# Attention maps of a two-layer transformer kernel: from one map at a time to pairs of maps in row and column groups of TensorE

## The reference, cut to what matters

```python
# HEADS 16, HD 4, per batch b, head h and side s (cut to its core)
S      = (q[b,h,s] @ k[b,h,s].T) * HD ** -0.5          # 1024 x 1024, contraction over 4
A[s]   = softmax(S, axis=-1)
out    = A[0] @ v[b,h] - lam * (A[1] @ v[b,h])          # v is 1024 x 8
out    = rms_norm(out) * w * (1 - LAMBDA_INIT)
x      = x + gate * (concat_heads(out) @ w_proj.T + b_proj)
```

## Time and profile before

| quantity | value |
|---|---|
| median of 3 runs | 3686.81 us (3684.1 to 3694.66) |
| the profiled execution: its time | 3684.8 us |
| the profiled execution: its span in the trace | 3683.0 us |
| mean granted clock of TensorE over the span | 0.962 of full speed |
| first max matmul of the attention maps | 89.15 us |
| last weighing matmuls of the attention maps | up to 1108.7 us |
| first matmul of `join_maps` | 1126.76 us |
| last step of `join_maps` | 1199.10 us |

### The profile page before, as it was taken

How to read it: one execution, slowest core, us unless ns; L and a number is a source line. 1 busy time by engine, 2 the same in 40 slices (tenths; PEclk the granted TensorE clock), 3 DMA queues, 4 the chain that set the end, 5 groups by cost and what they waited for, 6 DMA issues and landing times. The chain is left out here.

```text
span 3683.0 us, 71336 instructions
## 1 busy us (share of the span) xinstructions
PE 3280.8 (89%) x25164; PEld 1821.2 (49%) x25164; DVE 2741.0 (74%) x3715; ACT 2013.3 (55%) x2780; POOL 1119.2 (30%) x709
## 2 busy tenths in 40 slices
PE   4999999999995688888888888888889888869997
PEld 2222222222224455556555565656555565548886
DVE  2777777777753598979888797989898887946664
ACT  2455555555551366666667676766666676621111
POOL 2000000000001464645455454555464454610000
PEclk7899999999995799999999999999999999979999
DMA  3000000000002210011011001001110110100001
GB/s 114 11 16 15 14 15 15 15 15 15 15 14 93 66 29 24 29 48 34 18 35 48 24 29 54 29 24 29 53 29 23 29 35 21 32 23 1 0 0 29
DMA packets 70710, 107.05 MB, mean 29 GB/s; under 512 B 26790, under 2 KB 41012, under 8 KB 69684
## 3 DMA queue, kind: packets, MB, share of 16 engines
q1 hardware_dynamic: 69716, 104.37, 9.8%
q10 hardware_dynamic: 864, 0.79, 0.1%
HBM read 38.79 MB, written 15.73 MB: 15 GB/s over the span
## 5 line engine op out<-in xcount | busy, mean ns | idle before, releaser
L924 DVE TENSOR_REDUCE a_part_max<-a_ps_max 128x1 f32<-128x512 f32 x1024 | 683.2, 691 | 290.6 <-PE a_ps_max L846 288.7
L822 ACT ACTIVATE a_expT<-a_ps_scoresT 128x1024 f32<-128x1024 f32 x512 | 517.0, 1024 | 314.6 <-PE a_ps_scoresT L858 309.2
L1614 DVE STREAM_TRANSPOSE b_probsT<-b_probs 32x1024 f32<-32x1024 f32 x384 | 474.3, 1235 | 94.3 <-POOL b_probs L1240 85.2
L867 PE MATMUL a_ps_out<-a_expT,a_v_op 128*32 128x512 f32 x2048 | 537.6, 605 | 0.7 <-issue 0.5
L1216 POOL TENSOR_TENSOR b_turned_q<-b_rot_q,b_turned_q 128x1024 f32<-128x1024 f32 x96 | 226.8, 2363 | 711.3 <-DVE b_turned_q L1548 711.3
L846 PE MATMUL a_ps_max<-a_k_op,a_q_op 96*128 96x512 bf16 x1024 | 401.3, 392 | 25.7 <-DMA a_k_op<-terms_k 21.8
L846 PEld LDWEIGHTS a_ps_max<-a_k_op,a_q_op 96*128 96x128 bf16 x1024 | 98.3, 96 | 516.2 <-DVE a_part_max L924 428.6
L1441 PE MATMUL b_psD<-b_probsT,b_v 128*64 128x128 f32 x3072 | 337.8, 278 | 5.8 <-DVE b_probsT L1614 5.8
L1442 PE MATMUL b_psD<-b_probsT,b_v_back 128*64 128x128 f32 x3072 | 332.8, 274 | 0.0
L1456 PE MATMUL b_psD<-b_w_qkv,b_xs 128*128 (+1 forms) x384 | 211.3, 638 | 111.6 <-ACT b_outT L1305 111.6
L858 PE MATMUL a_ps_scoresT<-a_q_op,a_k_op 128*128 128x512 bf16 x1024 | 306.8, 380 | 0.0
(11 more groups left out here) (294 smaller groups left out, 5907.9 us busy)
## 6 DMA issues: line engine op xcount, KB each, us to landing
b_v_back<-b_v SPq DMA_DIRECT2D x96, 384.0 KB, 3.5
b_v_back<-b_v SPq DMA_DIRECT2D x96, 128.0 KB, 3.4
b_w_qkv<-L_ffn_Wqkv SPq DMA_DIRECT2D x6, 1536.0 KB
sums<-a_outT SPq DMA_DIRECT2D x512, 16.0 KB
j_got<-sums SPq DMA_DIRECT2D x16, 512.0 KB
a_q_op<-terms_q SPq DMA_DIRECT2D x64, 48.0 KB
a_k_op<-terms_k SPq DMA_DIRECT2D x64, 48.0 KB
b_w_o<-L_ffn_Wo SPq DMA_DIRECT2D x6, 512.0 KB
```

Source lines behind the costliest of these rows:

```text
L822: act.activation(expT[kt % RING][:], ps_scoresT[kt % 2][:], ACT.Exp, scale=SCALE_A).then_inc(exp_ready, 1)
L867: last_mm = pe.matmul(ps_out[lo:lo + 32, :], v_op[(u // 2) % 2][:, kt, :], expT[kt % RING][:, 512 * half:512 * half + 512], start=(kt < 2) ...
L924: dve.tensor_reduce(part_max[:, qt, half:half + 1], ps_max[half][:], AX.X, ALU.max).then_inc(max_taken, 1)
L1614: dve.transpose(probsT[rows, :, :, rows].rearrange("p c h q -> p h c q"), probs[rows]).then_inc(probsT_ready, 1)
```

## The change

Two maps, the two sides of one head, are now worked on together, as pair p of 32 (PAIRS_A). The parts:

- `q_op` and `k_op` hold, in each of the four groups of 32 partitions, 24 rows of data and the two maximum rows (or ones): groups 0 and 1 hold two copies of side 0, groups 2 and 3 two copies of side 1. Each matmul uses one group (24 or 26 rows), and the two matmuls of a burst, the two halves of 512 columns, use the two groups of one side and different PSUM banks.
- A burst of max matmuls fills 128 queries x 1024 keys of one side; DVE takes the maximum with one instruction over 1024 columns, already negated (L858 of the new kernel). The three small steps go; instead PE turns the pair's 16 columns in f32 into a corner of `ps_max[1]`, and DVE makes the two bf16 parts from it (L848, L850). SP sends eight rows per pair.
- scoresT of a key tile is four halves (two sides x two halves), in a ring of three banks; ACT takes them as a ring of two and one: 1024 columns, then 512, then 1024 ...
- The weighing of a key tile comes in two parts of 256 columns; in each part four matmuls go to the four column groups (side x half). `v_op` and POOL's copies go: `v_aug` is stored with 32 columns.
- PE's turn per key tile of a pair: max burst, scoresT burst of side 0, weighing part 0 of the tile two back, max burst, scoresT burst of side 1, weighing part 1.
- `ps_out` has no partial sums by parity any more. The stores go into SBUF (`joined`), and `join_maps` has neither its loads nor its two kinds of additions.
- All loops of the stage are written out instead of running as loops of the engines.

The core of the diff:

```diff
@@ join_maps @@
-                        sp.dma_start(got[n % 2][:, kind, side], sums[kind, side, b * HEADS_A:b * HEADS_A + HEADS_A, :, :, lo:lo + GROUP]
-                pool.tensor_tensor(numerators[n % 2][:], got[n % 2][:, 0, :, 0, :], got[n % 2][:, 0, :, 1, :], ALU.add).then_inc(numerators_ready, 1)
-                dve.tensor_tensor(denominators[n % 2][:], got[n % 2][:, 1, :, 0, :], got[n % 2][:, 1, :, 1, :], ALU.add).then_inc(denominators_ready, 1)
+                dve.tensor_tensor(mean[n % 2][:], joined[b][:, 0, :, lo:lo + GROUP], ps_inv[:], ALU.mult).then_inc(mean_ready, 1)
...
@@ attention_maps, SP @@
+            def rows(p):
+                slot = p % RING
+                sp.wait_ge(max_hi_ready, p + 1)
+                sp.wait_ge(max_lo_ready, p + 1)
+                for side in range(2):
+                    for copy in range(2):
+                        lo = group(side, copy) + ROWS
+                        sp.dma_start(q_op[slot][lo:lo + 1, :], max_hi[p % 2][T8 * side:T8 * side + T8, :]).then_inc(row_in[slot], 16)
+                        sp.dma_start(q_op[slot][lo + 1:lo + 2, :], max_lo[p % 2][T8 * side:T8 * side + T8, :]).then_inc(row_in[slot], 16)
...
@@ attention_maps, ACT @@
-                    act.activation(expT[kt % RING][:], ps_scoresT[kt % 2][:], ACT.Exp, scale=SCALE_A).then_inc(exp_ready, 1)
+            for e in range(EXPS):
+                first = 3 * (e // 2) + 2 * (e % 2)
+                size = min(2 - e % 2, HALVES * PAIRS_A - first)
...
+                act.activation(expT[:, to:to + 512 * size], ps_scoresT[:, at:at + 512 * size], ACT.Exp, scale=SCALE_A).then_inc(exp_ready, 1)
@@ attention_maps, PE @@
+            def max_scores_of(u):
+                p, qt, side = u // UNITS, u % UNITS // 2, u % 2
+                slot = p % RING
...
+                if u >= 2:
+                    pe.wait_ge(max_taken, u - 1)
+                if u % UNITS == 1 and p >= 1:
+                    pe.wait_ge(max_lo_ready, p)
                 for half in range(2):
+                    lo = group(side, half)
+                    last_mm = pe.matmul(ps_max[u % 2][:, 512 * half:512 * half + 512], q_op[slot][lo:lo + ROWS, P * qt:P * qt + P],
+                                        k_op[slot][lo:lo + ROWS, 512 * half:512 * half + 512], start=True, stop=True)
+                last_mm.then_inc(max_scores, 1)
+                if u % UNITS == 0 and p >= 1:
+                    turn_row(p - 1)
...
+            def scores(p, kt, side, place):
+                for half in range(2):
+                    n = HALVES * p + 4 * kt + place + half
+                    lo = group(side, half)
+                    if n >= 3:
+                        pe.wait_ge(exp_ready, exp_of(n - 3) + 1)
+                    pe.matmul(ps_scoresT[:, 512 * (n % 3):512 * (n % 3) + 512], k_op[slot][lo:lo + ROWS + 2, P * kt:P * kt + P],
+                              q_op[slot][lo:lo + ROWS + 2, 512 * half:512 * half + 512], start=True, stop=True).then_inc(scoresT_ready, 1)
...
+                for place, (side, half) in enumerate(((0, 0), (0, 1), (1, 0), (1, 1))):
+                    lo = group(side, half)
+                    at = 512 * ((n + place) % SLOTS) + 256 * part
+                    last_mm = pe.matmul(ps_out[lo:lo + 32, 256 * part:256 * part + 256], v_aug[:, b * T8 + kt, head, :], expT[:, at:at + 256],
+                                        start=(kt == 0 and part == 0), stop=(kt == T8 - 1), skip_group_check=True)
...
@@ attention_maps, DVE @@
+                dve.tensor_reduce(minus_max[p % 2][:, at:at + 1], ps_max[u % 2][:], AX.X, ALU.max, negate=True).then_inc(max_taken, 1)
+                if u % UNITS == 0 and p >= 1:
+                    row_out(p - 1)
```

More of the change, by code:

```diff
@@ L740, in _ @@
-            for M in range(3):
-                operands(M, M)
-            row(0, 0, 0)
-            def step(M, u, more, first=False):
-                if not first:
-                    sp.wait_ge(pv_done, T8 * M)
-                if more:
-                    operands(M + 3, (u + 3) % RING)
-                row(M + 1, (u + 1) % RING, (u + 1) % 2)
-                if not first:
-                    store(M - 1, (u + 1) % 2)
-            for u in range(RING):
-                step(u, u, True, u == 0)
@@ new lines, in _ @@
+            for p in range(RING - 1):
+                sp.wait_ge(ones_set, p + 1)
+                operands(p)
+            rows(0)
+            for p in range(PAIRS_A):
+                if p == 0:
+                    sp.wait_ge(ones_set, RING)
+                else:
+                    sp.wait_ge(pv_done, T8 * p)
+                if p + RING - 1 < PAIRS_A:
+                    operands(p + RING - 1)
+                if p >= 1:
+                    store(p - 1)
+                if p + 1 < PAIRS_A:
+                    rows(p + 1)
@@ L788, in _ @@
[L788 to L792 removed]
+                pool.memset(t[:], 1.0).then_inc(ones_set, 1)
         @block.scalar
         def _(act):
[L797 to L803 removed]
@@ L824, in _, with out_copy @@
[L824 to L832 removed]
+            def out_copy(p):
+                act.wait_ge(pv_done, T8 * (p + 1))
+                if p >= 2:
+                    act.wait_ge(out_sent[p % 2], 128 * (p // 2))
+                act.activation(outT[p % 2][:], ps_out[:], ACT.Copy).then_inc(out_held, 1)
@@ L834, in _ @@
+            out_copy(PAIRS_A - 1)
         @block.tensor
         def _(pe):
-            pe.wait_ge(cleared, 2 * RING + 2 + RING)
-            def max_scores_of(turn, slot, qt, first=False, halves=(0, 1)):
-                M = RING * turn + slot
-                if qt == 0 and 0 in halves:
-                    pe.wait_ge(operands_in[slot], 32 * (turn + 1))
-                for half in halves:
-                    if not (first and qt == 0):
-                        pe.wait_ge(max_taken, 2 * T8 * M + 2 * qt + half - 1)
-                    pe.matmul(ps_max[half][:], q_op[slot][0:ROW, P * qt:P * qt + P], k_op[slot][0:ROW, 512 * half:512 * half + 512],
-                              start=True, stop=True).then_inc(max_scores, 1)
```

307 lines of the change are left out of this document (110 added, 197 removed).

## The result

The changed kernel takes 3718.8 us (median of 4 runs, 3717.2 to 3721.8), the kernel before it 3685.5 beside it (4 runs, 3680.6 to 3694.7): ratio 1.0089, 95% interval 1.0067 to 1.011. The forecast was 3415, with a range from 3300 to 3540. It was wrong, and rival (c) is what happened.

The account below looks back on a forecast made before the run. PE's own row was taken to bound the attention-map stage (512 tiles x 1.955 = 1001 us); 250 us saved there plus 20 in the joining, 270 off 3684.8, gave 3415 us, range 3300 to 3540.

Parts of the forecast that it names:

- rival (c): Attention-map stage: TensorE stays at 1.2 GHz, a pair takes 33 us, the kernel gets slower at 3725 us; chance 0.05.
- The clock: Attention-map stage: granted clock 1.00, that is 2.4 GHz, after the first few us.
- The sum: Whole kernel: 250 us from the stage and 20 from the joining, off 3684.8, giving 3415 us.
- Row groups overlap: Max and scoresT bursts: two matmuls in different row groups run fully side by side, 0.22 us per burst.
- (a): Max and scoresT bursts: row groups do not overlap, bursts cost 0.44, +109, 3525 us; chance 0.2, mixtures included.
- PE per half tile: PE in the stage: 0.22 + 0.31 + 0.57 = 1.10 us per half key tile, 2.20 per pair's key tile.
- ACT's loop through three banks: scoresT ring: waits on ACT make four of six gaps 1.49 us, two 1.10; three key tiles take 8.16 us.
- DVE: Maxima in the stage: 1.22 us per 1024 columns, two per key tile are 2.4 of 2.7, so room remains.
- (b): Stage: the interlock with ACT is softer and DVE bounds it, 20.0 us per pair, -105, 3310 us; chance 0.13.
- Rows by DMA: Eight row DMAs per pair: 6.9 us, landing at 9.2 before use at 9.4; counted as nothing, only 0.2 cover.
- Start: Start of the stage: operands ready at 81, first scoresT at 110 against 112.42, 2 us gained.
- Joining: Joining of the maps: dropped loads and additions and cheaper clips save 19 to 21 us, taken as 20.

Follow-up runs that it names:

- the warmed-up run: The changed kernel with 40 whole-array matmuls added once, in the ninth pair ahead of one scoresT burst; 3714.3 us, ratio 1.0083 to the kernel before.

## Why the prediction was wrong, step by step

- **The clock: the step that failed.** The sum took 2.4 GHz for the whole stage ("Clock 1.00 after the first few us"). Against rival (c) I had put: "at 1.2 GHz PE's row is full again, as it was when the clock rose here". The row is full (98%) and the clock stays low. The kernel before falls to the same clock with a full row when its matmuls contract over 24 rows. What I had taken from the earlier trace rows was how long PE is busy; what mattered too was what its matmuls work on, and that stands in the shapes of the earlier trace rows: 96x512 and 128x512. I had written that the new bursts fill only half of the rows, and gave it 0.05. The price, from the stretch at 2.4 GHz: 32 x (32.4 - 22.6) = 314 us. Without it the changed kernel would stand at some 3719 - 314 = 3405, beside my 3415; that is worked out from one pair, not run. That the two lie only 10 us apart is in part luck: the pair is 0.7 shorter than summed (22 us less), the joining 8 and the rest of the program 3 longer.
- **Row groups overlap: right.** 0.21 per burst at 2.4 GHz, 0.40 at 1.2 GHz; (a) is out. The Trainium skill (TensorE: Matmul & The Clock Gate, Measured speedup vs the span model) gives 3.07 times for four row groups, which would have made 0.28 of a burst, as an estimate; two groups show none of that loss here. Four row groups were not run.
- **PE per half tile, and ACT's loop through three banks: right.** 1.11 for 1.10, and 1.49 or 1.53 for 1.49. The pair is 22.6 for 23.3, turn included.
- **DVE:** 1.22 per reduction as taken, and in the changed kernel it waits for PE. (b) is out: at 2.4 GHz the pair is 22.6, not 20.0.
- **Rows by DMA:** right in that PE waits for none of them once the stage runs; only the first pair's wait shows (1.8 us at 107.75). But its pairs take 32 us. At 2.4 GHz the cover was as thin as I had said: in the warmed-up run the next pair's first burst started behind the rows, at 407.83, and the half tile before it took 1.19 (from 406.64) in place of 1.11. The load of that burst's weights:

```profile
407.83 0.09 PEld L777 LDWEIGHTS a_ps_max<-a_k_op,a_q_op 24*128 24x128 bf16 x2 [0.49 <-DMA a_q_op<-a_max_lo]
```

- **Start:** first product at 80.5 (predicted 81), first scoresT at 108.2 (110).
- **Joining: mis-sized.** Predicted 20, measured 12. From the last copy to the first product it takes 8.3 us instead of 18.0: 9.7 saved, where I had 12.5. The clips take 0.43, as said. But the time from that first product to the first turned_q step of the local blocks on POOL fell only from 118.5 to 116.0, where clips and additions should have brought 6 to 8. The view of that line, first of the kernel before, then of the changed one (count; shortest, median and longest in ns; first to last start):

```profile
L1216 POOL TENSOR_TENSOR b_turned_q<-b_rot_q,b_turned_q x96: 2343/2362/2381, 1245.3 to 3211.0; 128x1024 f32<-128x1024 f32 x96
```

```profile
L1144 POOL TENSOR_TENSOR b_turned_q<-b_rot_q,b_turned_q x96: 2344/2365/2377, 1277.4 to 3244.0; 128x1024 f32<-128x1024 f32 x96
```

  What DVE's steps gave back mostly became its waiting: its last step of the joining comes 69.8 us after that first product, where it was 72.3, and in between it now waits 6.2 us for PE's denominators of the later groups of tokens, where it had waited 1.3, and 5.0 in place of 2.3 for the first product behind them. The longest of these for the denominators:

```profile
1190.16 0.96 DVE L509 RECIPROCAL j_inv<-j_ps_den 128x128 f32<-128x128 f32 x1 [3.01 <-PE j_ps_den L596]
```

- **(c)'s own sum** was 3725, measured 3719: the pair is 32.4, not 33 (-18), the joining short by 8, the rest 3 longer.

## What to carry to other kernels

Before trading wide matmuls for packed narrow ones, read the granted clock of the stretch and the contraction rows of the matmuls that ran while it was up; a full row of PE (98% here) is not enough to count on 2.4 GHz. Where the clock is low, padding with zeros can pay: here 128 rows for 26 in the scoresT matmuls alone brought 3719 down to 3486, at the cost of more streaming. And when a forecast hangs on one state for a whole stage, give its loss the chance that the evidence allows: one stretch in which many things differ is no evidence for one of them.

## What the runs showed of the hardware

- With PE busy in 98 to 100% of the stretch, the granted clock was 0.50 (1.2 GHz) for all of the stage where max and scoresT matmuls worked on 24 to 26 rows, packed or one after the other, or on 64; it was 1.00 (2.4 GHz) where max worked on 96 or 128 rows and scoresT on 128, or scoresT alone on 128, and 0.98 with max alone on 128. Rows of zeros count: the padded runs, in which most rows of the queries hold zeros, read 1.00 as well, and the kernel before fell to 0.50 when they were left out. The weighing, over 128 rows of f32 in two or four groups of 32 columns, takes about half of PE's time in the changed kernel (603.51 to 604.53 of a half tile of 1.98) and in the kernel before over 24 rows; it did not lift the clock there, and why it does not count like the others stays open.
- One whole-array matmul more per half tile of 2.5 us did not lift it either (0.50).
- Once up, it stayed up for 30 us of packed bursts in one place, until behind a wait of 0.70 us, and for 3 us in another, which had gaps. Whether such a gap is needed for the fall stays open, and so does whether the rows count by degrees.
- Two row groups stream side by side at either clock: a burst of two matmuls moves PE on by 0.21 us at 2.4 GHz, where one matmul takes 0.22, and by 0.40 at 1.2 GHz, where one takes 0.41 (two in one row group 0.82).
